# Two of thirty-two recurrence units multiplied in eight plain products instead of seven summed ones, in a state-space plus LSTM kernel on one Trainium2 core

## What is computed

```
x = r + layernorm(gelu(conv(layernorm(r), K)))   # K from the state-space parameters
z = layernorm(x)
f = sigmoid(z @ wf.T + c @ uf.T + bf)
i = sigmoid(z @ wi.T + c @ ui.T + bi)
g = tanh   (z @ wc.T + c @ uc.T + bc)
c = f * c + i * g                                 # scanned over the first axis
out = x + layernorm(tanh(z @ wo.T + c_final @ uo.T + bo))
```

## Time and profile before

| what | value |
|---|---|
| median of 3 runs | 2634.09 us (2632.4 to 2635.8) |
| profiled execution, its own time | 2635.06 us |
| its span, first to last instruction | 2633.4 us |
| mean granted clock | 0.986 |
| busy: PE, DVE, ACT, POOL | 2524.9, 1834.9, 1627.5, 1127.6 us |
| chain that ended last, by engine | PE 84%, DVE 4%, ACT 3%, DMA 2% |
| HBM traffic | 180 GB/s over the span |

### The profile page before, as it was taken

The page is one execution under the profiler, slowest core; times in us unless marked ns, Lnnn a source line. Parts: engine busy times, 40 slices in busy tenths (PEclk is TensorE's granted clock), DMA queues, the critical chain, the costliest instruction groups (busy, mean ns, idle before and its releaser), DMA issues.

```text
span 2633.4 us, 57587 instructions
## 1 busy us (share of the span) xinstructions
PE 2524.9 (96%) x22659; PEld 2203.9 (84%) x22659; DVE 1834.9 (70%) x3411; ACT 1627.5 (62%) x3013; POOL 1127.6 (43%) x1437
## 2 busy tenths in 40 slices
PE   5599999997999999999999999999999999999998
PEld 4378888886788888888888888888888888888887
DVE  7865656558886777767777887776677764467667
ACT  8766767666665555555557665555555553379777
POOL 7878677724332223222234432322223220068667
PEclk9799999998999999999999999999999999999999
DMA  8879778889664565445655755544556432489998
GB/s 353 322 236 335 263 264 296 296 299 331 162 179 117 138 147 157 117 114 138 151 157 157 208 146 144 162 119 115 136 134 171 117 85 49 161 339 351 368 358 346
DMA packets 507551, 542.52 MB, mean 206 GB/s; under 512 B 273936, under 2 KB 412944, under 8 KB 488720
## 3 DMA queue, kind: packets, MB, share of 16 engines
q1 hardware_dynamic: 507280, 538.85, 65.7%
HBM read 292.88 MB, written 180.88 MB: 180 GB/s over the span
## 4 chain that ended last, share of the span: by engine, by line
PE 84%; DVE 4%; ACT 3%; DMA 2%; issue 1%; POOL 1%; SPq 1%; DVEq 0%; ACTq 0%; POOLq 0%
PE bank L2178 31%; PE bank L2188 29%; PE bank L2234 8%; PE bank L2067 4%; PE bank L2017 3%; PE bank L2053 3%; PE bank L2075 3%; PE bank L2029 2%; PE bank L2209 2%; DVE big L1859 1%; PE bank L2037 1%; ACT big L1360 1%; DVE big L1916 1%; DMA x1d<-big 1%; DVE big L1902 0%
## 5 line engine op out<-in xcount | busy, mean ns | idle before, releaser
L2178 PE MATMUL bank<-big 128*128 128x256 f16 x8064 | 1081.3, 274 | 18.3 <-ACT big L1406 7.9
L2188 PE MATMUL bank<-big 128*128 128x256 f16 x7056 | 962.5, 273 | 0.0
L2178 PEld LDWEIGHTS bank<-big 128*128 128x128 f16 x8064 | 791.7, 98 | 116.1 <-ACT big L1406 9.6
L2188 PEld LDWEIGHTS bank<-big 128*128 128x128 f16 x7056 | 690.4, 98 | 79.9
L1042 POOL TENSOR_SCALAR big<-big 128x1 f32<-128x1 f32 x253 | 108.1, 427 | 1088.0 <-DVE big L1706 810.9
L1916 DVE TENSOR_TENSOR big<-bank,big 128x512 f32<-128x512 f32 x256 | 174.9, 683 | 197.6 <-PE bank L2188 193.5
L2234 PE MATMUL bank<-big 128*128 128x256 f16 x2688 | 295.3, 273 | 4.4 <-ACT bank L1340 4.0
L1316 ACT ACTIVATE big<-big 128x512 f32<-128x512 f32 x384 | 289.6, 803 | 12.6 <-DVE big L1916 12.6
L2234 PEld LDWEIGHTS bank<-big 128*128 128x128 f16 x2688 | 262.4, 98 | 36.9 <-ACT bank L1340 4.9
L1902 DVE TENSOR_TENSOR big<-bank,big 128x512 f32<-128x512 f32 x256 | 176.1, 688 | 143.1 <-PE bank L2188 119.4
L1248 ACT ACTIVATE big<-big 128x512 f32<-128x512 f32 x256 | 206.4, 808 | 105.1 <-POOL big L1044 101.6
(11 more groups left out here) (236 smaller groups left out, 3715.2 us busy)
## 6 DMA issues: line engine op xcount, KB each, us to landing
xtd<-big SPq DMA_DIRECT2D x60, 1024.0 KB, 6.7
big<-xr SPq DMA_DIRECT2D x16, 2048.0 KB, 9.2
big<-xg SPq DMA_DIRECT2D x64, 512.0 KB, 7.7
big<-kpad SPq DMA_DIRECT2D x32, 1024.0 KB, 12.3
yd<-big SPq DMA_DIRECT2D x16, 2048.0 KB, 16.8
big<-x SPq DMA_DIRECT2D x128, 256.0 KB, 3.2
x1d<-big SPq DMA_DIRECT2D x128, 256.0 KB, 3.2
big<-x1d SPq DMA_DIRECT2D x64, 512.0 KB, 8.5
```

The source lines that it names most:

```text
L2178: ins = e.matmul(o, WX[2 * g + lw][:, q, kt, 128 * a:128 * a + 128], slot[u % 2][:, part, lx, k0 + kt, :], start=(first and kt == 0 and (l ...
L2188: ins = e.matmul(o, WC[2 * g + lw][:, q, kt, 128 * a:128 * a + 128], cc[unit(u)[1] % 2][:, qc, lx, kt, :], start=False, stop=end, skip_gro ...
```

## The change

For units 0 and 1, and for the four head pairs that belong to them (m = 34, 35, 50, 51), the 7-product form is replaced by 8 plain block products. Two plain parts of the rows suffice, so no sums of rows are made, split, turned, or stored for these units, and the slots hold half as much. The plain form needs W12 itself, which before was overwritten by a sum; it is kept as an eighth weight part of the four matrices wf, wi, wc and wo, cut at one more place in the convolution stage (`lo`/`hi` with f = 7), stored in `w12d` (256 KB each) and loaded again. A plain group has 48 matmuls, 24 for bank A and 24 for bank B, with no copy in between; ACT's gate functions read the two banks directly (`gates_plain`) and DVE adds nothing. The tables of unit 1's preparation move from groups 0 to 6 to groups 0 and 1. SP loads the weights of gate g ahead of unit 1's x, and unit 2's x right behind unit 1's last transposes.

Core of the diff:

```diff
-                behind = (7, 8, 9, 11, 12, 13, 14) if n == 2 else (4, 5, 6, 8, 9, 11, 13)
+                behind = (7, 9, 10, 11, 12, 13, 14, 8) if n == 2 else (4, 6, 7, 8, 9, 11, 13, 5) if n % 4 == 2 else (4, 5, 6, 8, 9, 11, 13)
...
+PLAIN_UNITS = 2
+PLAIN_PAIRS = tuple(m for m in range(PAIRS) if head_unit(m // 2) < PLAIN_UNITS)
+PLAIN = tuple(range(6 * PLAIN_UNITS)) + tuple(GROUPS + m for m in PLAIN_PAIRS)
...
-    1: {"dve": ((0, 0), (0, 0), (0, 0), (0, 0), (0, 2), (0, 3), (2, 1), (2, 3), (2, 3), (3, 2), (3, 3), (4, 3), (4, 3), (5, 3), (5, 3), (5, 3), (5, 3), (5, 3)),
+    1: {"dve": ((0, 0), (0, 0), (0, 0), (0, 0), (0, 1), (0, 1), (0, 2), (0, 3), (0, 3), (9, 0), (1, 0), (9, 0), (9, 0), (9, 0), (1, 1), (1, 1), (9, 0), (9, 0)),
...
-                else:
+                    turn(6)
+                    turn(7)
+                    for c in CHUNKS:
+                        load_x1(2, c)
+                    store_xt(0)
+                    load_WC(5)
+                    store_xt(1)
+                    return
...
+            w.wait_ge(s["w12"], 16 * 4)
+            e.dma_start(f16(x1_at + 4096, 1024).rearrange("p (g x) -> p g x", g=2), w12d[0:2].rearrange("g p l x -> p g (l x)")).then_inc(s["w12"], 16)
...
+            def gates_plain(n):
+                u, gi = divmod(n, 6)
+                a, g = divmod(gi, 3)
+                w.wait_ge(s["yc"], 3)
+                room(n)
+                bs = bias0 if unit(u)[0] == 0 else bias
+                for r in range(2):
+                    w.wait_ge(s[("pa", "pb")[r]], n + 1)
+                    e.activation(zt[g][:, r::2, :], (bank_a(n), bank_b(n))[r][:, :].rearrange("p (q t) -> p q t", q=2), ACT.Tanh if g == 2 else ACT.Sigmoid,
+                                 bias=bs[:, g, a + 2 * r:a + 2 * r + 1], scale=inv[g]).then_inc(s["ga"], 1)
...
-            w.wait_ge(s["accs"], 16 * 3)
-            first_sums(ss, 0)
...
+            def plain(n, r, o, sem):
...
+                for h in range(2):
+                    w.wait_ge(s[f"xq{h}"], 32 * u)
+                    for k in range(2):
+                        for kt in range(2):
+                            for lw, lx in PARTS:
...
+                                ins = e.matmul(o[:, 256 * h:256 * h + 256], part[:, kt, 128 * a:128 * a + 128], slot[u % 2][:, h, lx, 2 * k + kt, :],
...
-                    step(n, 4, A[:, 256:512], True)
-                    step(n, 1, A[:, 0:256], False, "pa")
-                if n:
-                    w.wait_ge(s["k5"], n)
+                    if n in PLAIN:
+                        whole(n, 0, A, "pa")
+                    else:
+                        step(n, 4, A[:, 256:512], True)
+                        step(n, 1, A[:, 0:256], False, "pa")
+                if n and n - 1 not in PLAIN:
+                    w.wait_ge(s["k5"], before(n))
```

396 lines of the change are left out of this document (244 added, 152 removed).

## The result

| | before | after |
|---|---|---|
| median (9 runs each) | 2634.31 us (2632.37 to 2635.8) | 2639.85 us (2638.32 to 2642.95) |
| ratio, 95% interval | | 1.0024 (1.0016 to 1.0033) |
| profiled execution, its span | 2635.06, 2633.4 us | 2642.95, 2641.2 us |

I had forecast 2624.4 us, with a range of 2617 to 2632. The changed kernel is 5.5 us slower than before and lies outside the range.

What follows compares the result with a forecast made beforehand. PE's matmul count was taken to bound the kernel except in a dip with 24.6 us of waits and half clock. There 12.6 us won, less 2.6 and 0.3 lost, gives 9.7: 2624.4 us, range 2617 to 2632.

Steps and rivals of the forecast that it cites:

- more weights to cut: Convolution stage: cutting four more parts on ACT and DVE, mostly hidden, costs 0.3 us, up to 3 kept possible.
- a stage that ends later than 584: Sign of being wrong: the convolution stage ending later than 584 us.
- the dip: PE's stretch with waits and half clock through units 0 and 1: unit 2's effective start moves from 681.8 to 669.2, winning 12.6 us.
- Unit 0: Effective start 602.1 us including 2.0 for half clock; 288 matmuls without waits for weights, copies or gates; end at 633.5.
- Unit 1: Transposes ready between 631 and 635.3 us, needed at 633.5: no wait taken, bound 1.8 plus 1.6 of clock; end at 664.9.
- Unit 2: Last add at 648.0 us, usable 19.6 later at 667.6; stall 2.7 and clock 1.6, effective start 669.2, bounds 664.9 and 674.
- DVE, busy almost throughout, comes late: Sign of being wrong: DVE, while it prepares unit 2, is what comes late.
- The head: Four head pairs get 24 more matmuls, paid in full because PE has no gap there: +2.6 us.
- A: Rival: the stall before unit 2 does not occur; start 664.9, gain 14.0 us, time 2620.1; chance 0.20.
- C: Rival: unit 1's x lands late, at 614 to 616 us; unit 2 starts at 672 to 675, time 2627 to 2630; chance 0.18.
- D: Rival: unit 2's chain is not shortened, PE starts it at 681 as before; costs stand alone, +2.9, 2637.0 us; chance 0.14.

Runs made afterwards that it cites:

- cut_only_early: cut_only with POOL's last weight difference of iteration 2 made before its second norm, not its fourth: 2636.73 us, 1.0010 to the kernel before.
- sum_early: The changed kernel with POOL's last weight difference of iteration 2 made before its second norm, not its fourth: 2633.59 us, 0.9998 to before.
- no_eighth: The changed kernel without the eighth weight part; plain products take a stored sum of weights instead, so values differ: 2631.06 us, 0.9988 to before.
- wc_last: early_add with all six state-weight loads on SP behind unit 1's transposes and the loads of unit 2's x: 2634.84 us, 1.0002 to before.
- y2_behind: early_add with SP's load of unit 2's convolution rows behind unit 1's first two transposes: 2632.34 us, 0.9992 to before.
- early_add: sum_early with DVE's last addition for unit 2 moved ahead of the state's first part: 2633.11 us, 0.9996 to before.
- turns_first: early_add with unit 2's four second-half transposes ahead of unit 3's loads on SP, in order part 1, 0, 2, 3: 2637.88 us, 1.0013 to before.
- warm: turn_swap_act with 22 more matmuls, into a bank nothing reads, in PE's pauses ahead of unit 0: 2628.52 us, 0.9982 to before.
- cut_only: The kernel before with the changed convolution stage: eighth weight part cut and stored, never loaded: 2643.12 us, 1.0036 to before.
- turn_swap: early_add with unit 2's second-half transposes in order part 1, 0, 2, 3, behind unit 3's row load, ahead of its x loads: 2629.00 us, 0.9981 to before.
- turn_swap_act: turn_swap with ACT's first normalisation for unit 3 behind its copy for PE instead of ahead: 2628.39 us, 0.9979 to before.

## Why the prediction was wrong, step by step

**The failed step: "+0.3" for more weights to cut, "and keep up to 3".** It was 10.4 us at the stage's end. I priced ACT's and DVE's cuts, and looked whether they had slack; they had (cut_only_early: 1.7 us at the stage's end for all of it, within the 0.3 to 3 that I gave). In that step I named neither POOL nor its queue. The change made the fourth difference wait for the eighth part's cut, and moved it behind three norms. In the trace before, POOL starts its differences at 172.7 us; three of them (4.0) and three norms of 4.8 put the fourth at 191.1, and ACT's L1241 cut that part at 187.4. All of it stood there to be read. sum_early shows what the place alone costs: with it mended the kernel is the same as before (0.9998) and not 0.24% slower. The prediction's own sign of being wrong, a stage that ends later than 584, is what came.

**The second failed step: the dip, "681.8 - 669.2 = 12.6 won".** It won 7.1. Without this miss sum_early would stand inside the range; it stands at 2633.59 us, and even no_eighth, which cuts nothing, at 2631.06. The missing 5.5 are, from the parts below: the start of unit 0 0.7, the gates and the rest of unit 0 0.6, unit 1, mostly by its two waits, 2.2, the wait before unit 2 1.3 and its clock 0.7.

**Unit 0.** Start: 602.1 forecast, 602.8 measured on the old clock (610.20 + 3.0 of half clock - 10.4). Its end: 633.5 forecast, 634.8 measured, with 0.46 us for ACT's gates, which I had excluded. Right but for size; the clock's 2.0 was 3.0.

**Unit 1.** "I take no wait; the bound is 1.8 plus 1.6 of clock." The bound came true: 1.8 us in two waits in the changed kernel (with no loss of clock), 2.4 and 1.9 of clock in no_eighth. End: 664.9 forecast, 668.4 measured. The step missed what the loads on SP do to the transposes: the third store holds SP 6.22 us in front of the first pair, and the second pair, behind two loads of state weights, takes 6.02. With all six of these loads behind the transposes (wc_last) the wait is gone; with only the store set free (y2_behind) it is not.

**Unit 2.** Addition 648.0 forecast, 652.2 measured; from there 19.6 and 20.3 us. The addition follows group 8, as I said, but group 8 itself started at 647.3 and not at 644.0 (PE's row: 657.7 - 10.4), 3.3 late by what units 0 and 1 had lost; the rest is DVE, where L1915's pair took 1.82 us and I had 0.88. But early_add shows that an earlier addition would not have helped. The chain behind it is of two parts, SP's list and DVE's lows, and I had only measured its length, not what it consists of. I had misread it too: "2.15 each" is the mean of one transpose that held SP 4.27 us, behind the load of unit 3's rows, and three of 1.25 to 1.55; part 1 landed at 680.0 and not at 677.8, so the trace before has 21.8 us from add to usable where I had 19.6. That DVE, busy almost throughout, comes late was one of my signs of being wrong, and early_add's rows show it. Effective start 669.2 forecast, 674.7 measured (681.8 less the 7.1 won).

**The head.** +2.6 forecast. The trace shows 1.31 us for each two plain pairs, 2.6 in all, and 0.2 more: right.

**The rivals.** A did not occur in the changed kernel; turns_first starts unit 2 without a wait, at 670.8 us, but PE then waits 8.24 us from 676.2 on. C (unit 1 late, its x behind weights) is half right: unit 1 was late, by its transposes. Its first piece of x was there by 622.06 - 10.4 = 611.7, when DVE's add takes it, near my 611. The Trainium skill's rule (DMA: Bandwidth & Descriptors, section Queues, rings and completion order), that each DMA engine consumes the descriptors of one issuer in ring order, from which I took that loads behind cannot delay x, is again not borne out cleanly: from the issue at 607.61 to that landing the windows carry 5.3 MB, while 3.4 MB were issued up to the first piece of x, and the stores in front, which may still have been under way, are 1.0 MB. These are sums over the 16 engines, and the rule speaks of each engine, so they do not refute it. D, the other side, reached 2637.0 by its own mechanism; the actual 2639.85 came by none that I had.

**Sum.** Forecast -12.6 + 2.6 + 0.3 = -9.7. In the traces: -7.1 in the dip, +2.8 in the head and +0.6 behind it, +10.4 in the stage, +1.0 at 1364 to 1496 us: +7.8 (each rounded), of which the medians show 5.5.

**What stays open.** The 1.0 us in two places near 1410 and 1495 us is in the changed kernel and, with 0.6 to 1.5 us, in every other one with plain units except warm, which loses nothing there; nor do cut_only and cut_only_early. So plain units do not bring it about by themselves. PE waits there for ACT's copy a little longer (1.27 instead of 0.51 at the first place; 0.50 in warm), ACT for a transpose, and SP's four transposes take 6.2 and 6.3 us in the changed kernel instead of 5.4. Nothing in the change touches these units. No experiment was made on it.

## What to carry to other kernels

An edit that makes one more thing wait must be followed on the engine that waits, with everything that its list holds in front and behind: here the slack of two busy engines was weighed and the third engine, whose queue decided, was not. A row that merges several transfers is taken apart before its mean is used as a price. Where the work that PE waited for ran through a shared queue, moving one transfer mostly shifted the wait to the next unit; only putting first the transpose that the first product needs, with nothing but the load of unit 3's rows between it and the first half (turn_swap, 4.1 us), took most of a wait away without giving it back. The version turn_swap_act, the change with the edits of sum_early, early_add and turn_swap and its own, is 0.21% faster than the kernel before (ratio 0.9979, 0.9971 to 0.9988).
